# Six of eight experts computed on sorted rows instead of on every token

## The reference, cut to what is computed

```python
# x is (8 batches, 128, 128), fp32
f   = advection_diffusion_step(x, A_grid, B_grid, dt)     # finite differences along both axes, then relu
h   = layernorm over features, then norm over tokens, then * gamma + beta   # gamma, beta from a small net on subject ids
h_flat = h.reshape(1024, 128)                              # 1,024 tokens
probs  = softmax(h_flat @ router_w)                        # (1024, 8)
gates, idx = top_k(probs, 2); gates = gates / gates.sum(-1)
hid  = relu(einsum('nd,edf->nef', h_flat, exp_w1) + exp_b1)  # 8 experts, 128 -> 512
eout = einsum('nef,efd->ned', hid, exp_w2) + exp_b2          # 512 -> 128
y    = einsum('ned,ne->nd', eout, combine)                 # combine holds the two gates of each token
return f + y
```

## Time and profile before

| | us |
|---|---|
| median of 3 runs (lowest, highest) | 118.12 (117.46, 118.76) |
| the profiled execution | 117.98 |
| its span, first to last instruction | 116.2 |
| PE busy | 111.0 (96%) |
| DVE, ACT, POOL busy | 90.6, 78.0, 9.1 |
| mean granted TensorE clock | 0.996 |

### The profile page before, as it was taken

The page is one execution under the profiler, slowest core; times in us unless marked ns, Lnnn a source line. Parts: engine busy times, 40 slices in busy tenths (PEclk is TensorE's granted clock), DMA queues, the critical chain, the costliest instruction groups (busy, mean ns, idle before and its releaser), DMA issues.

```text
span 116.2 us, 1540 instructions
## 1 busy us (share of the span) xinstructions
PE 111.0 (96%) x511; PEld 86.3 (74%) x511; DVE 90.6 (78%) x198; ACT 78.0 (67%) x108; POOL 9.1 (8%) x18
## 2 busy tenths in 40 slices
PE   5999999999999999999999999999999999999960
PEld 2589897458546788888888888888888888888850
DVE  0696996589990896999869967996799499788881
ACT  2643547845625997777777777777777777777800
POOL 1578040000000000000000000000000000000040
PEclk9999999999999999999999999999999999999998
DMA  3999993000000650220400320040005000400005
GB/s 93 297 328 404 412 412 135 0 3 0 0 0 11 158 203 6 89 92 0 181 0 0 110 73 0 6 176 4 0 0 181 0 0 27 159 0 0 0 0 181
DMA packets 4583, 10.86 MB, mean 93 GB/s; under 512 B 800, under 2 KB 1888, under 8 KB 4576
## 3 DMA queue, kind: packets, MB, share of 16 engines
q1 hardware_dynamic: 4144, 10.43, 25.5%
q10 hardware_dynamic: 432, 0.34, 0.9%
HBM read 10.21 MB, written 0.56 MB: 93 GB/s over the span
## 4 chain that ended last, share of the span: by engine, by line
PE 96%; DVE 1%; DVEq 0%; issue 0%
PE zt L698 11%; PE zt L700 11%; PE zt L699 11%; PE yt L692 6%; PE aux L722 6%; PE aux L726 6%; PE aux L723 6%; PE zt L679 5%; PE yt L726 5%; PE yt L722 5%; PE yt L723 5%; PE zt L559 3%; PE zt L574 2%; PE yt L671 1%; PE zt L686 1%; PE aux L634 1%
## 5 line engine op out<-in xcount | busy, mean ns | idle before, releaser
L529 ACT ACTIVATE hid_hi<-zt,pv 128x1024 fp32r<-128x1024 f32 x27 | 30.2, 1119 | 17.4 <-PE zt L700 17.2
L1025 DVE TENSOR_TENSOR hid_lo<-hid,hid_hi 128x1024 fp32r<-128x1024 f32 x27 | 33.0, 1221 | 10.0 <-issue 5.4
L534 ACT ACTIVATE hid<-zt,pv 128x1024 f32<-128x1024 f32 x27 | 29.9, 1108 | 0.0
L698 PE MATMUL zt<-h_hi,ws 128*128 128x512 f32 x56 | 22.7, 406 | 0.0
L700 PE MATMUL zt<-h_lo,ws 128*128 128x512 f32 x56 | 21.8, 390 | 0.0
L699 PE MATMUL zt<-h_hi,ws 128*128 128x512 f32 x56 | 21.8, 389 | 0.0
L698 PEld LDWEIGHTS zt<-h_hi,ws 128*128 128x128 f32 x56 | 10.5, 188 | 2.9 <-issue 0.5
L699 PEld LDWEIGHTS zt<-h_hi,ws 128*128 128x128 f32 x56 | 10.5, 188 | 2.5 <-issue 0.5
L700 PEld LDWEIGHTS zt<-h_lo,ws 128*128 128x128 f32 x56 | 10.5, 188 | 2.2
L723 PE MATMUL aux<-hid_hi,ws 128*128 128x512 f32 (+1 forms) x32 | 12.0, 376 | 0.0
L726 PE MATMUL aux<-hid_lo,ws 128*128 128x512 f32 (+1 forms) x32 | 12.0, 376 | 0.0
(11 more groups left out here) (147 smaller groups left out, 148.1 us busy)
## 6 DMA issues: line engine op xcount, KB each, us to landing
we<-in_exp_w_dram SPq DMA_DIRECT2D x8, 512.0 KB, 8.8
gate_all<-gates_dram SPq DMA_DIRECT2D x8, 512.0 KB, 3.6
f<-in_x_dram SPq DMA_DIRECT2D x2, 256.0 KB, 4.4
ft<-in_x_exchanged_dram SPq DMA_DIRECT2D x2, 256.0 KB, 5.3
out_dram<-acc SPq DMA_DIRECT2D x1, 256.0 KB, 2.1
out_dram<-acc SPq DMA_DIRECT2D x2, 128.0 KB, 2.0
first<-d_difference_dt_ids_dram ACTq DMA_DIRECT2D x1, 137.0 KB, 3.1
gn<-in_grids_dram SPq DMA_DIRECT2D x1, 128.0 KB, 3.3
```

Of the source, the lines that this page charges most:

```text
L529: act.activation(hid_hi[:, c, :], zt[c % 2][:], ACT.Relu, bias=bias).then_inc(hi_ready, 1)
L534: act.activation(hid[:, c, :], zt[c % 2][:], ACT.Relu, bias=bias).then_inc(hid_ready, 1)
L698: pe.matmul(zt[c % 2][:, tok], w_hi, h_hi[:, tok], start=True, stop=False)
L1025: v.tensor_tensor(hid_lo[:, c, :], hid[:, c, :], hid_hi[:, c, :].bitcast(F32), ALU.subtract).then_inc(lo_ready, 1)
```

## The change

Experts 0 and 1 stay dense: they are computed on all tokens, both in plain fp32 now, with tokens on the partitions in layer 2 (16 calls of 128 columns for each half instead of 4 of 512). Experts 2 to 7 get only the tokens routed to them:

1. DVE finds the two experts of each token with `max` and `max_index` of the logits, and builds a mask; PE sums the mask into each token's rank within its expert (`ranks`) and the experts' counts (`counts`).
2. `rows_dram` has 49 blocks of 128 rows of 130 words: eight for each of six experts, and one spare. SP fills all of it with zero rows (`spare_row`, one DMA of 6,272 rows of 520 bytes), once `fills_ready` says that POOL has prepared that row. Two more DMAs clear `sums_dram`.
3. POOL scatters 16 times 128 token rows (512 B of `h`, place, gate) to their places in `rows_dram` with indirect DMAs.
4. DVE makes a list of 21 codes, the blocks that are in use and spare blocks for the rest (`tile_codes`); SP reads each into a register.
5. For each of the 21 tiles, SP loads the expert's 128x1156 weights (592 KB; 512 KB of matrices and the biases, b2 spread over the partitions) and the 128 rows; PE transposes the rows, DVE copies them, PE makes four 128-column calls of layer 1, ACT four relus, PE four calls of layer 2, DVE applies the gate, and POOL scatters the 128 result rows to `sums_dram`.
6. SP waits for all scatters, loads the sums in eight DMAs, DVE adds them, and four DMAs store the output.

The split into high and low parts and its work on ACT and DVE are gone, as is the gates' way through DRAM.

The core of the diff (the routing arithmetic on DVE is cut):

```diff
+DENSE = 2
+ROUTED = E - DENSE
+BLOCKS = T // P
+TILES = (TOPK * T + ROUTED * (P - 1)) // P
+SPARE = ROUTED * BLOCKS
+ROW = P + 2
+W_SLOTS = 5
+ROW_SLOTS = 8
+PIECES = 4
...
         @block.sync
-            for e in range(E):
-                load(we[:, e], exp_w[e], w_in[e])
...
+            for e in range(DENSE):
+                load(we[:, e], exp_w[ROUTED + e], w_in[e])
+                if e == 0:
+                    load(rc[:], routing, routing_in)
+            sp.wait_ge(fills_ready, 3)
+            sp.dma_start(rows_dram.rearrange("(q p) w -> p q w", p=P),
+                         spare_row[:].unsqueeze(1).broadcast_to((P, SPARE + 1, ROW))).then_inc(filled, 16)
...
+            sp.wait_ge(code_ready, 1)
+            codes = [sp.value_load(code[i:i + 1, 0:1], min_val=0, max_val=SPARE) for i in range(TILES)]
+
+            def tile_weights(i):
+
+                if i >= W_SLOTS:
+                    sp.wait_ge(tile_yg, i - W_SLOTS + 1)
+                sp.dma_start(wt[:, i % W_SLOTS, :],
+                             exp_w[bass.ds(codes[i] >> 3, 1)].rearrange("o p w -> p (o w)")).then_inc(
+                                 tile_w_in[i % W_SLOTS], 16)
+
+            def tile_rows(i):
+
+                if i >= ROW_SLOTS:
+                    sp.wait_ge(tile_out[i % ROW_SLOTS], 16 * (i // ROW_SLOTS))
+                sp.dma_start(rt[:, i % ROW_SLOTS, :],
+                             rows_dram[bass.ds(codes[i] * P, P), :]).then_inc(tile_rows_in[i % ROW_SLOTS], 16)
+
+            for i in range(W_SLOTS):
+                tile_weights(i)
+            sp.wait_ge(rows_out, 16 * B * TOPK)
+            for i in range(TILES):
+                tile_rows(i)
+                if i + W_SLOTS - 2 < TILES and i >= 2:
+                    tile_weights(i + W_SLOTS - 2)
...
         @block.gpsimd
+            pool.wait_ge(filled, 16)
...
+                        pool.indirect_dma_start(
+                            rows_dram, bass.IndirectOffsetOnAxis(ap=row_i[:, b, k:k + 1], axis=0), h_row[:, k, b, :],
+                            None, bounds_check=(SPARE + 1) * P - 1, oob_is_err=False).then_inc(rows_out, 16)
...
+            for i in range(TILES):
+                n = i % ROW_SLOTS
+                pool.wait_ge(tile_rows_in[n], 16 * (i // ROW_SLOTS + 1))
+                pool.wait_ge(tile_yg, i + 1)
+                pool.indirect_dma_start(
+                    sums_dram, bass.IndirectOffsetOnAxis(ap=rt[:, n, ID_AT:ID_AT + 1].bitcast(I32), axis=0),
+                    yg_t[:, n, :], None, bounds_check=TOPK * T - 1, oob_is_err=False).then_inc(tile_out[n], 16)
...
         @block.tensor
+            def tile_transposed(i):
+
+                pe.wait_ge(tile_rows_in[i % ROW_SLOTS], 16 * (i // ROW_SLOTS + 1))
+                if i >= 2:
+                    pe.wait_ge(tile_xT, i - 1)
+                pe.transpose(xT_ps[i % 2], rt[:, i % ROW_SLOTS, 0:P], ident).then_inc(tile_xT_ps, 1)
...
+            tile_transposed(0)
+            for i in range(TILES):
+                tile_layer1(i)
+                if i + 1 < TILES:
+                    tile_transposed(i + 1)
+                if i > 0:
+                    tile_layer2(i - 1)
+            tile_layer2(TILES - 1)
...
         @block.vector
+            tile_columns(0)
+            for i in range(TILES):
+                if i + 1 < TILES:
+                    tile_columns(i + 1)
+                tile_gated(i)
```

More of the change, by code:

```diff
@@ L341, in _ @@
+            for n in range(PIECES):
+                two = slice(n * B // PIECES, (n + 1) * B // PIECES)
+                sp.wait_ge(out_ready, n + 1)
+                sp.dma_start(out[:, two, :], acc[:, two, :]).then_inc(out_done, 16)
+            sp.wait_ge(out_done, 16 * PIECES)
         @block.gpsimd
@@ L547, in _ @@
-            for e in range(1, E):
+            gate_exponent(0)
+            hidden(0, 1, 0)
+            token_rows(1)
+            hidden(0, 1, 1)
+            gate_exponent(1)
+            hidden(0, 1, 2)
+            hidden(0, 1, 3)
+            for e in range(1, DENSE):
+                act.wait_ge(w_in[e], 16)
+                for n in range(HALVES):
+                    act.wait_ge(y_ready, (e - 1) * HALVES + n + 1)
+                    for c in range(C):
+                        hidden(e, n, c)
@@ new lines, in layer1_by_pairs, with layer2 @@
+                last.then_inc(z_ready, 1)
+            def layer2(e, n, c):
+                g = (e * HALVES + n) * C + c
+                pe.wait_ge(hid_ready, g + 1)
+                for k in range(BH):
+                    tok = slice((n * BH + k) * P, (n * BH + k + 1) * P)
+                    last = pe.matmul(y_d[e][n][:, k * P:(k + 1) * P], hid[:, c, tok], w2(e, c),
+                                     start=(c == 0 and k == 0),
+                                     stop=(c == C - 1), skip_group_check=True)
+                if c == C - 1:
+                    last.then_inc(y_ready, 1)
@@ L756, in _, with tile_layer2 @@
+            def tile_layer2(i):
+                if i >= 2:
+                    pe.wait_ge(tile_yg, i - 1)
+                for c in range(C):
+                    pe.wait_ge(tile_hid, C * i + c + 1)
+                    last = pe.matmul(y_t[i % 2], hid_t[:, i % 2, c, :],
+                                     wt[:, i % W_SLOTS, W2_AT + c * P:W2_AT + (c + 1) * P], start=(c == 0),
+                                     stop=(c == C - 1))
+                last.then_inc(tile_y, 1)
             pe.wait_ge(warm_ready, 1)
@@ L1091, in _ @@
[L1091 to L1095 removed]
+            row_numbers(0)
+            shares(0)
+            logit_tops(1)
+            choices(1)
+            logit_gap(1)
+            row_numbers(1)
+            shares(1)
+            tile_codes()
+            dense_gates(0)
+            dense_gates(1)
+            for e in range(DENSE):
+                for n in range(HALVES):
+                    add_biases(e, n)
+                    add_expert(e, n)
@@ new lines, in _ @@
+            tile_columns(0)
+            for i in range(TILES):
+                if i + 1 < TILES:
+                    tile_columns(i + 1)
+                tile_gated(i)
+            for n in range(PIECES):
+                two = slice(n * B // PIECES, (n + 1) * B // PIECES)
+                v.wait_ge(sums_in[n], 16 * TOPK)
+                v.wait_ge(acc_done, B * DENSE)
+                then(v.tensor_tensor(acc[:, two, :], acc[:, two, :], sums[:, 0, two, :], ALU.add))
+                v.tensor_tensor(acc[:, two, :], acc[:, two, :], sums[:, 1, two, :], ALU.add).then_inc(out_ready, 1)
```

706 lines of the change are left out of this document (355 added, 351 removed).

## The result

| | before | changed |
|---|---|---|
| time, median of 4 runs, us | 118.0 (117.46 to 118.76) | 213.19 (211.22 to 213.85) |
| ratio, 95% interval | 1 | 1.801 (1.788 to 1.814) |
| span of the profiled execution, us | 116.2 | 209.4 |
| its mean granted clock | 1.00 | 0.67 |

The changed kernel is 80% slower. The forecast was 191 with a range of 155 to 224. The profiled execution took 211.22, 1.8 on top of its span, as counted. Every ratio here compares fast executions alone: those more than 1.5% above the fastest of their kernel are left out of it.

A forecast was written before the change was run, and what follows sets the result against it. TensorE was taken to bound the kernel before, a rows' loop over one tile the changed one. Terms: 61 + 5.3 + 96 + 15 + 12 = 189 us of span, 1.8 on top: 191 us, range 155 to 224.

The forecast's parts named there:

- S: Start of the tiles, once PE's dense part, the fill and POOL's token scatters are through: 61 us.
- first gated result: Transpose, copy, two layers 1 and one layer 2 of the first tiles: 5.3 us.
- sixteen periods: Results 1 to 16 of the tile loop, at a period of 6.0 us each: 96 us.
- last four: Four more results at the pace of PE waiting for DVE, 3.75 us each: 15 us.
- tail: After the tiles: last scatter, loads of the sums, two additions and store: 12 us.
- The loop on SP: Tile loads: each gated result waits for rows issued after the result before; period 5.55 us at full clock, chance 0.78.
- R = 3.95: In each tile turn, from SP's weights issue to the landing of the rows queued behind them: 3.95 us.
- The rest of a period: From the rows' landing to SP's next issue: transpose, layer 2, gating and waits, 1.6 us at the full clock.
- The clock: PE's clock over the tiles: period 5.55 us at the full level, 6.4 at the low, middle taken as 6.0.
- POOL at 3 us each: Rival: indirect DMAs hold POOL 3 us or more each and POOL sets the pace; 220 us, chance 0.10.
- The hand-off: Rival: PE waiting for DVE between layer 2 and next layer 1 sets the tiles' pace; 145 us, chance 0.09.
- TensorE stays the bound: Rival: tiles follow PE at 1.9 us each, 110 us; chance 0.02 for faster, 0.01 for within 1%.

The follow-up runs named there:

- e1: Changed kernel with SP issuing the rows ahead of the weights in each turn, the wait for the gated result kept in front of both: 170.37 us.
- e2: Changed kernel with eight row loads issued at once, each row buffer loaded again once its scatter has read it: 144.18 us.
- e4: Changed kernel, order kept, plus unread matmuls on PE, 40 before the first tile and five in each turn: 194.13 us.
- b3: b2 with eight codes read before the tiles and 13 among them, row loads ahead of weights, a row buffer per tile, eight weight buffers: 115.49 us.
- e6: Changed kernel with SP reading five codes, each followed by its weights' load, and the other sixteen afterwards: 205.24 us.
- e5: Changed kernel with the fill of the row blocks written in 3,640-byte pieces instead of 520: 208.0 us.
- e3: e2 with DVE copying the columns of tile i+2 ahead of the gating of tile i: 138.33 us.
- b2: e3, e5 and e6 combined, plus later row reloads, bridging matmuls, sums' loads split with ACT, twelve weight buffers, earlier first-half row numbers and shares: 120.47 us, ratio 1.008.

## Why the prediction was right, and where its sizes were off

The sign, the mechanism and the range held. The sum of the span, step by step (each as the time from the mark before):

| step | predicted | measured | off |
|---|---|---|---|
| S, first transpose | 61 | 65.35 | +4.4 |
| first gated result | 5.3 | 6.9 | +1.6 |
| sixteen periods | 96 | 112.6 | +16.6 |
| last four | 15 | 11.6 | −3.4 |
| tail | 12 | 13.0 | +1.0 |
| span | 189.3 | 209.4 | +20.1 |

- **The loop on SP.** Right, place and count. SP waited 16 times for the gated result. e1 shows the bytes ahead of the rows, e2 the whole loop, e4 that it does not need the low clock. By "HWDGE ordering" in the Trainium skill ("DMA: Bandwidth & Descriptors") each DMA engine consumes a ring's descriptors in order, so rows issued behind weights come behind them; e1 agrees, 1.82 us against 3.42.
- **R = 3.95.** Right: 4.18 in the mean, 3.74 to 4.25 in all turns but the first (5.54). 16 × 0.23 = 3.7 us of the miss.
- **The rest of a period.** Mis-sized by 0.3 at the full and 0.4 at the low clock: 1.89 and 2.85 instead of 1.6 and 2.45. In the turn above 0.27 go by until layer 2 starts (0.2 taken), layer 2 takes 1.91 with its last matmul's end (1.66 taken, from starts alone), and SP issues 0.20 after the gating (0.05 taken); against that, DVE follows PE within 0.11 (0.2 taken). 6.4 us of the miss.
- **The clock.** I took the middle of the two levels, for want of a row. In all sixteen turns the transpose and layer 2 ran at the low level: 16 × 0.4 = 6.4 us. The section "Why this matters for your kernels" of the Trainium skill's "TensorE: Matmul & The Clock Gate" has loops with few rows and a DMA wait in each turn swing between the levels. e1 agrees, with 0.50 from 80 to 90 us and 1.00 from 95 to 110. The changed kernel swung only once, at its start, and then stayed at 0.50 from 80 to 185 us; e2's turns of 2.83 had 1.00 throughout. The low level all through was to cost some 10 us more than my sum; the turns give 6.4 of it.
- **S.** The fill's landing (36.6, 37 taken), the scatter's price and PE's dense part (54.2, 55 taken) were right within 1 us; POOL was through at 59.1 instead of 57.8: +1.3. Wrong were two covers. SP's register reads were called hidden, for nothing to 0.43 us each; they cost 0.6. That moved the weights onto the last scatter's landing: 4.2 us from POOL's end (5.2 from its issue) instead of 2.1, +2.1. The last 1.0 I had struck off as hidden, and it was not.
- **The first result.** 6.9 us, where 4.0 was priced at the full and 6.4 at the low clock: it was 0.50 until about 70 us, most of that way.
- **The last four.** 11.6 us is four times the 2.9 of the full level only by chance. Between the gated results lie 4.75, 2.92, 3.00 and 0.91 us: one turn at the low level (4.6 taken), two at the full (2.9 taken), and a last one that is no full turn, since no layer 1 stands in it. My sum counted four hand-off turns where there are three.
- **The rivals.** POOL at 3 us each is out (1.27). The hand-off was not what happened, but it is the state of e2 once the loop is gone, 2.83 us in the mean, 2.90 in the steady part. That its 145 us meet e2's 144.18 is luck: it was summed with turns of 3.3 (9.8 us too much over twenty), against a first transpose at 65.2 instead of 61 and a first result after 8.1 us instead of 4. "TensorE stays the bound" took all the repairs of b3 and then gave 115, not 110: the first transpose came at 57.9 instead of 56, the tiles took 42.9 instead of 40, and behind PE's end stood 12.6 us instead of 12.

## What to carry to other kernels

Where an engine's queue carries two streams, one that waits for buffers and one that is wanted next, write down what stands in front of each issue: the number of buffers says nothing if the queue's order spans one tile. Every repair here exposed the next head of a queue (a load behind a wait, then a reload behind a scatter's landing, then loads behind register reads), so after each the waits have to be read again. Before work is taken off a busy engine by sorting, sum what the sorting adds in front and behind: here, with the tiles mended, 9 us in front of them, 3 in them and 9 behind took 21 of the 24 that TensorE gained.

## What the runs showed of the hardware

- **Register reads.** A read of one word from SBUF into a register of SP holds its queue 0.6 us, by the gaps in that queue: 12.6 us for 21, 9.6 for 16. The Trainium skill ("DMA: Bandwidth & Descriptors", Latency and other measured facts) gives a floor of about 600 ns for `tensor_load`, and the gaps agree.
- **Indirect DMAs.** 128 rows of 520 bytes hold POOL 0.97 us, and 0.30 pass before the next one, in every kernel here (a few take up to 1.15); the first of a series takes 1.19.
- **Landing.** A scatter lands 2.1 to 2.5 us after its issue on quiet DMA engines and later beside loads of weights. The last token scatter took 2.45 in e6 (DMA share 0.11 from 56 to 60 us), 5.2 in the changed kernel (0.97 and more), 4.7 in e5 and 5.2 in b3. The result scatters took 3.6 in the median of the changed kernel and 4.5 in e3, and the first one of b2 6.0.
- **Small pieces.** 3.26 MB in 520-byte pieces took 20.7 us, in 3,640-byte pieces 11.6, each with the same two clears of 512 KB issued behind it. SP's queue felt it too: issuing these two clears took it 13.6 us behind the small pieces and 1.8 us behind the large ones.
- **The clock.** In turns of 7.03 us, with PE busy 12.2 of 20 us and waiting 1.6 to 2.1 us for rows in all but the first, it was 0.50 for more than 100 us. The same loop with unread matmuls in its wait had 0.89, e1's turns of 4.50 had both levels, and turns of 2.83 us had 1.00.
